# First K and Q projections of the attention moved into the last tile of the first FFN

## The reference, cut to what matters

```
x = L0_attn_x                                # (16, 256, 256) f32
x = x + 0.5 * ffn(layernorm(x), W_up, W_gate, W_down)
x = x + attn(layernorm(x), Wq, Wk, Wv, Wo, head_scale)
x = x + 0.5 * ffn(layernorm(x), W_up, W_gate, W_down)

ffn:  up, gate = x @ wu.T, x @ wg.T          # weights rounded to -1, 0, 1 times a scale, 1024 hidden
      return (silu(up) * gate) @ wd.T
attn: q, k = rotary(x @ Wq), rotary(x @ Wk)  # 16 heads, 4 KV heads of 128, causal
      p = softmax(q @ k.T / sqrt(128))
      return ((p @ v) * head_scale) @ Wo     # 16 sequences of 256 tokens
```

## Time and profile before

| what | us |
|---|---|
| median of 3 runs | 1092.58 |
| lowest and highest of the 3 | 1091.23, 1092.96 |
| the profiled execution | 1092.94 |
| its span in the profile | 1091.1 |
| PE busy in the span | 1070.3 |
| DVE busy in the span | 925.4 |
| ACT busy in the span | 815.4 |
| POOL busy in the span | 713.5 |

### The profile page before, as it was taken

How to read it: one execution, slowest core, us unless ns; L and a number is a source line. 1 busy time by engine, 2 the same in 40 slices (tenths; PEclk the granted TensorE clock), 3 DMA queues, 4 the chain that set the end, 5 groups by cost and what they waited for, 6 DMA issues and landing times.

```text
span 1091.1 us, 26889 instructions
## 1 busy us (share of the span) xinstructions
PE 1070.3 (98%) x8517; PEld 844.1 (77%) x8517; DVE 925.4 (85%) x2313; ACT 815.4 (75%) x2038; POOL 713.5 (65%) x906
## 2 busy tenths in 40 slices
PE   7999999899999999999999999999999999999998
PEld 5556566688888888888888888888888887656565
DVE  6787876899999999999999999999999997433333
ACT  6787887788788787887878878788787785444443
POOL 2566675776777777777777767777677774444443
PEclk9999999999999999999999999999999999999999
DMA  9522332234434344343433434334434343100101
GB/s 347 156 48 40 58 59 37 40 71 89 74 74 76 72 82 82 72 78 65 90 70 72 82 73 81 67 72 82 82 72 76 72 83 73 30 19 19 38 19 38
DMA packets 262166, 79.93 MB, mean 73 GB/s; under 512 B 249328, under 2 KB 260848, under 8 KB 261872
## 3 DMA queue, kind: packets, MB, share of 16 engines
q1 hardware_dynamic: 261696, 79.19, 34.9%
q10 hardware_dynamic: 432, 0.27, 0.1%
HBM read 12.85 MB, written 4.19 MB: 16 GB/s over the span
## 4 chain that ended last, share of the span: by engine, by line
PE 71%; issue 10%; ACT 6%; POOL 6%; DVE 5%; DMA 1%; POOLq 0%; SPq 0%; DVEq 0%; ACTq 0%
PE bank L750 45%; PE bank L808 14%; POOL SCR L409 5%; PE bank L709 4%; PE bank L719 4%; PE bank L739 4%; ACT SCR L619 2%; DVE ARENA L1128 1%; DVE SCR L1089 1%; ACT SCR L492 1%; ACT ARENA L626 1%; DMA X<-in_wg 1%; DVE bank L1108 1%; ACT SCR L507 1%; ACT SCR L517 1%
## 5 line engine op out<-in xcount | busy, mean ns | idle before, releaser
L440 POOL TENSOR_SCALAR SCR<-SCR,RI 128x128 f32<-128x128 f32 (+1 forms) x512 | 309.6, 605 | 44.0 <-DVE RI L1124 3.8
L619 ACT ACTIVATE SCR<-bank,NM 128x128 f32<-128x128 f32 (+1 forms) x512 | 208.2, 419 | 124.3 <-DVE NM L1108 124.3
L425 POOL TENSOR_TENSOR SCR<-SCR 128x512 f32<-128x512 f32 x160 | 203.1, 1269 | 149.4 <-DVE SCR L1089 146.8
L409 POOL TENSOR_TENSOR SCR<-SCR 128x512 f16<-128x512 f32 x128 | 152.7, 1194 | 156.5 <-ACT SCR L507 155.4
L808 PE MATMUL bank<-SCR 128*128 128x128 f32 (+1 forms) x1024 | 193.9, 332 | 4.8 <-ACT SCR L619 4.8
L948 DVE SCALAR_TENSOR_TENSOR SCR<-SCR,CS,bank 128x512 f32<-128x512 f32 x128 | 95.1, 743 | 119.3 <-PE bank L719 98.5
L591 ACT COPY SCR<-bank 64x512 f32<-64x512 f32 x320 | 185.5, 580 | 12.5 <-PE bank L750 6.5
L1128 DVE TENSOR_TENSOR ARENA<-SCR,ARENA 128x768 f16<-128x768 f32 x128 | 187.9, 1468 | 5.5 <-ACT ARENA L626 4.9
L750 PE MATMUL bank<-WOH,ARENA 128*128 128x256 f16 x1024 | 188.3, 273 | 0.8 <-DVE X L1151 0.8
L1108 DVE CUSTOM_DVE_ANT_0 bank<-bank,MASK,SCQ 128x128 f32<-128x128 f32 (+1 forms) x512 | 183.0, 416 | 0.9
L517 ACT ACTIVATE SCR<-bank,SU 128x512 f32<-128x512 f32 x128 | 87.7, 685 | 112.1 <-PE bank L709 110.7
(11 more groups left out here) (120 smaller groups left out, 1651.0 us busy)
## 6 DMA issues: line engine op xcount, KB each, us to landing
out<-X SPq DMA_DIRECT2D x7, 512.0 KB, 2.9
X<-in_x SPq DMA_DIRECT2D x1, 2560.0 KB, 11.2
ARENA<-in_wq SPq DMA_DIRECT2D x1, 2048.0 KB, 13.5
ARENA<-in_wo SPq DMA_DIRECT2D x1, 2048.0 KB, 18.6
SCR<-ARENA SPq DMA_TRANSPOSE x128, 3.6
X<-in_x SPq DMA_DIRECT2D x3, 512.0 KB, 9.9
X<-in_wu SPq DMA_DIRECT2D x2, 512.0 KB, 5.8
X<-in_wg SPq DMA_DIRECT2D x2, 512.0 KB, 7.7
```

The lines of the kernel that those rows point to most:

```text
L409: gp.tensor_tensor(HL[:, f % 4, :], H32[:, f % 2, :], HH[:, f % 4, :], ALU.subtract).then_inc(s["hl_done"], 1)
L425: gp.tensor_tensor(dst, M1[:, m, :], M2[:, m, :], ALU.add).then_inc(add, 1)
L440: last = gp.tensor_scalar(EX[:, par, lo:hi], EX[:, par, lo:hi], RI[:, par, c:c + 1], PS, ALU.mult, ALU.mult)
L619: last = act.activation(EX[:, par, 384 * hh + lo:384 * hh + hi], SBK[hh][:, lo:hi], ACT.Exp, bias=NM[:, par, c:c + 1], scale=-1.0, accum_o ...
```

## The change

K0 and Q0 are projected in the last tile, behind up and gate of pieces 4 and 5, into banks 6 and 7 (`PJ0`). Their swaps follow on ACT in pieces 5 and 6, their multiplications on DVE in pieces 6 and 7; the addition of K0 stands on POOL ahead of piece 7's remainder, that of Q0 behind it. This needs M1 and M2 apart from SG and H32: they go to the addresses of the raw K and V weights, and QF, EX, PT, XN2 and the stores of the second FFN move too. So all casts must be done before the last tile: the fourth quarters of Q, K, V and O move into tiles 4 to 6. The exponential table is loaded ahead of the last `high`. In batch 0, scores of step 0 stand ahead of the Q projection of step 2, the down projections of (7, 5), (7, 6) and (7, 7) go one each into steps 2, 3 and 4, and the residual of tile 7 goes to step 4. The low half of norm job 14 goes to step 0 of batch 0; the job's earlier parts move up by a piece (statistics at piece 2, centering at 4). New waits: the first exponential waits for the last remainder, the first two turns of probabilities for down projections, and values of steps 5 and 6 for the residual.

```
-        CAST_HI = [(2, 2, 5, 6)] * 3 + [(0, 0, 1, 2)]
-        CAST_LO = [(2, 5, 6, 7)] * 3 + [(1, 2, 2, 4)]
+        CASTS_HI = {(4, 2): [(Q, 0), (K, 0)], (4, 5): [(V, 0), (K, 3), (V, 3)], (4, 6): [(O, 0)],
+                    (5, 2): [(Q, 1), (K, 1)], (5, 5): [(V, 1), (Q, 3)], (5, 6): [(O, 1)],
+                    (6, 2): [(Q, 2), (K, 2)], (6, 5): [(V, 2), (O, 3)], (6, 6): [(O, 2)]}
...
-                norm_job(2 * n, n - 1, at + 3, at + 5, at + 5, at + 6)
+                norm_job(2 * n, n - 1, at + 2, at + 4, at + 5, at + FC)
@@ SP, turns of the probabilities
+                            if e < 2:
+                                sp.wait_ge(ff[0]["down_done"], FC * TILES - 1 + e)
@@ POOL, piece
+                if layer == 0 and n == TILES - 1 and f == FC - 1:
+                    rope_add(0, 0, KF[:, 0, :], 0)
                 gp.wait_ge(s["hh_done"], FC * n + f + 1)
@@ ACT, piece
+                    if n == TILES - 1 and f in (5, 6):
+                        act.wait_ge(proj, f - 4)
+                        act.wait_ge(w_ready, 4 * len(CUTS))
+                        rope_swap(f - 5, f - 5, PJ0[f - 5])
@@ ACT, between the FFN and the batches
+            act.activation(WARM[:, 1:2], NEGHALF[:, 0:1], ACT.Exp)
             high(0, TILES - 1, FC - 1)
@@ PE, ffn
-                    if layer == 0 and isinstance(n, int) and (n, f) == (TILES - 1, FC - 1):
-                        pe.wait_ge(w_ready, 3 * len(CUTS) + 2)
-                        pe.wait_ge(ff[0]["silu_done"], FC * TILES - 1)
...
-                        project_qk(PJ[0], WKH, WKL, 0, 0)
+                    if layer == 0 and (n, f) == (TILES - 1, 4):
+                        pe.wait_ge(w_ready, 4 * len(CUTS))
+                        pe.wait_ge(ln_x[1], 16 * (TILES - 2))
+                        project_qk(PJ0[0], WKH, WKL, 0, 0)
+                    if layer == 0 and (n, f) == (TILES - 1, 5):
+                        project_qk(PJ0[1], WQH, WQL, 0, 0)
@@ PE, batch
+                    if first and i == 2:
+                        pe.wait_ge(ff[0]["h_done"], FC * TILES)
+                        scores(0, 0, 0)
...
-                            for f in range(FC - LAG, FC):
-                                down(0, TILES - 1, f)
...
+                    if first and 2 <= i < 2 + LAG:
+                        down(0, TILES - 1, FC - LAG + i - 2)
...
+                        if first and i in (5, 6):
+                            pe.wait_ge(ff[0]["x_done"], SUB * TILES)
@@ DVE, piece
+                    if n == TILES - 1 and f >= FC - 2:
+                        if f == FC - 2:
+                            ve.wait_ge(tab_in, 32)
+                        rope_mul(f - FC + 2, f - FC + 2, PJ0[f - FC + 2])
@@ DVE, batch
+                    if first:
+                        norm_lo(2 * TILES - 2)
...
-                    if isinstance(b, int) and (b, i) == (0, 0):
-
+                    if isinstance(b, int) and (b, i) == (0, 4):
                         residual(0, TILES - 1)
```

More of the change, by code:

```diff
@@ L419, in ffn @@
                     piece(layer, n, f)
[L421 to L425, removed]
             def rows_rstd(e):
@@ L506, in high, with rope_swap @@
                 wait(act, s["down_done"], j - 3)
-                act.copy(HH[:, f % 4, :], H32[:, f % 2, :]).then_inc(s["hh_done"], 1)
+                act.copy(HH[layer][:, f % 4, :], H32[layer][:, f % 2, :]).then_inc(s["hh_done"], 1)
+            def rope_swap(r, m, src):
+                wait(act, add, r - 1)
+                for d, s in ((0, 64), (64, 0)):
+                    last = act.copy(M2[d:d + 64, m, :], src[s:s + 64, :])
+                last.then_inc(swap, 1)
             def piece(layer, n, f):
@@ L583, in _ @@
                 ffn(0, n)
+            act.activation(WARM[:, 1:2], NEGHALF[:, 0:1], ACT.Exp)
             high(0, TILES - 1, FC - 1)
-            def rope_swap(r, m):
-                wait(act, add, r - 1)
-                for d, s in ((0, 64), (64, 0)):
-                    last = act.copy(M2[d:d + 64, m, :], PJ[m][s:s + 64, :])
-                last.then_inc(swap, 1)
             def batch(b):
@@ L597, in batch @@
                     u, t = 2 * b + g, PAIRS * b + i
-                    if real(b, i, 0):
+                    if real(b, i, 0) and not (isinstance(b, int) and b + i == 0):
                         r, m = 5 * u + 1 + k, (5 * g + 1 + k) % 2
@@ L939, in residual, with rope_mul @@
                                             ALU.mult, ALU.add).then_inc(s["x_done"], 1)
+            def rope_mul(r, m, src):
+                wait(ve, add, r - 1)
+                ve.wait_ge(swap, r + 1)
+                two = lambda a: a.rearrange("p (h n) -> p h n", h=2)
+                for dst, a, tb in ((M1[:, m, :], src[:, :], COS), (M2[:, m, :], M2[:, m, :], SIN)):
+                    last = ve.tensor_tensor(two(dst), two(a), tb[:, :].unsqueeze(1).to_broadcast([P, 2, SEQ]), ALU.mult)
+                last.then_inc(mul, 1)
             def piece(layer, n, f, prev):
@@ L988, in weights @@
                     scales()
[L989 to L990 removed]
+                for i, part in CASTS_LO.get((n, f), ()):
                         raw, hi, lo, size, c = CUTS[i]
[L992 to L993 removed]
+                        cols = slice(part * size, (part + 1) * size)
+                        ve.wait_ge(w_hi, HI_ORDER.index((i, part)) + 1)
                         ve.scalar_tensor_tensor(flat(lo)[:, cols], raw[:, cols], AFAC[:, c:c + 1],
@@ L1077, in _ @@
                 ffn(0, n, n > 0)
-            ve.wait_ge(tab_in, 32)
-            def rope_mul(r, m):
-                wait(ve, add, r - 1)
-                ve.wait_ge(swap, r + 1)
-                two = lambda a: a.rearrange("p (h n) -> p h n", h=2)
-                for dst, src, tb in ((M1[:, m, :], PJ[m][:, :], COS), (M2[:, m, :], M2[:, m, :], SIN)):
-                    last = ve.tensor_tensor(two(dst), two(src), tb[:, :].unsqueeze(1).to_broadcast([P, 2, SEQ]), ALU.mult)
-                last.then_inc(mul, 1)
             def batch(b):
@@ L1110, in batch @@
                             last.then_inc(mx, 1)
-                    if real(b, i, 0):
-                        rope_mul(r, m)
-                    if isinstance(b, int) and (b, i) == (0, 0):
+                    if real(b, i, 0) and not first:
+                        rope_mul(r, m, PJ[m])
+                    if isinstance(b, int) and (b, i) == (0, 4):
                         residual(0, TILES - 1)
```

81 lines of the change are left out of this document (38 added, 43 removed).

## The result

| what | before | after |
|---|---|---|
| median of 17 runs each, us | 1092.52 | 1094.87 |
| lowest and highest | 1091.21, 1093.61 | 1093.58, 1095.68 |
| the profiled execution | 1092.94 | 1094.21 |
| its span | 1091.1 | 1092.4 |

The ratio of after to before is 1.0021, 95% interval 1.0015 to 1.0028: 1.6 to 3.1 us slower. The forecast was 1094.2.

A forecast was written before the change was run, and what follows sets the result against it. PE bounds the attention; at the seam its idle time counts, DVE and ACT setting the pace after the first scores. Casts 0, seam 0, clock +1.6 on the median 1092.58 gave 1094.2, range 1090.8 to 1096.0.

The forecast's parts named there:

- The casts: Four more casts in each of tiles 4 to 6, none in tile 7: hidden in ACT's and DVE's slack, 0 us.
- the 1.09 us stall: PE's down projection at 173.29 waits for the residual of tile 6; claimed to go, up of (7, 4) 1.09 earlier.
- s0: Start of the first scores on PE, released by POOL's addition of Q0: forecast 192.15, before 194.65.
- one such collision: DVE's low half of norm job 14 overlapping a POOL remainder ahead of the first scores: POOL loses 0.9 us.
- From s0 to the mark: From first scores to maxima of step 3, with Q2 and tile 7's residual on the path: 18.8 us, 16.3 before.
- The seam at the full clock: From the first FFN's last tile to the maxima of step 3, without a clock fall: 0 us change.
- The clock: PE's pause of 4.5 us ahead of the first scores drops the clock to 1.2 GHz: +1.6 us.
- the row at 15 to 20 us: Profile window with a PE pause of 1.79 us; up and gate took 3.35 instead of 1.73, source of the 1.6.
- the clock didn't hold: Rival: the clock holds through PE's pause and the seam is a wash, 1092.6 (1091.7 to 1093.7); chance 0.27.
- the lead didn't come through: Rival: shorter DVE and ACT path behind the first scores keeps their lead, 1090.1 to 1091.1; chance 0.13, 0.04 for more.
- the slower mechanism: Rival: three POOL collisions, first scores at 193.2, they and Q2 at half speed: +1.1 + 2.7 = 3.8, 1096.4; chance 0.11.
- the casts hid: Rival claimed the opposite: casts make PE wait in tiles 4 to 6, 3 x 1.24 less 1.1, 1095.2; chance 0.05.

The follow-up runs named there:

- e7: Kernel before with only the casts moved into tiles 4 to 6 and PE's wait before the first K projection for all casts; ratio to before 0.9984.
- e8: Changed kernel with DVE's low half of norm job 14 behind the rotary products of Q1 instead of ahead of them; ratio to before 1.0002.
- e4: Changed kernel with POOL's addition of Q0 ahead of the remainder of (7, 7) instead of behind it; ratio to before 1.0002.
- e1: Changed kernel with 20 unread identity matmuls on PE in the pause between the first Q1 projection and the first scores; ratio to before 1.0007.
- e10: e2 with 14 unread identity matmuls on PE in the pause between Q2 and the first scores; ratio to before 0.9986.
- e2: Changed kernel with Q2 projected on PE ahead of the first scores instead of behind them; ratio to before 1.0000.
- e3: Changed kernel with down projections of (7, 5) and (7, 6) ahead of the first scores, Q2 still behind; median 1094.48 us, ratio to before 1.0007.
- e5: Changed kernel with down (7, 5), Q2 and down (7, 6) ahead of the first scores, Q0's addition ahead of the last remainder; 1089.80 us, ratio to before 0.9967.
- e6: e5 with the residual of tile 7 at step 3 and the last down projection right behind the first scores; 1089.58 us, ratio to before 0.9966.

## Why the prediction was right, and where its sizes were off

**The casts cost nothing: right.** No wait in tiles 4 to 6, and the 1.09 us stall gone. What I had missed is that they are worth 0.87 us more in the old arrangement (e7), 0.65 of it because the K projection, by the reading above, waited for a silu that came late behind ACT's norm work. The changed kernel has no use for it, since K0 goes to a bank of its own.

**s0: too early by 0.68.** Forecast was 192.15 - 162.94 = 29.21 from up of (7, 0), it came at 29.89. The step that failed is "I take one such collision, 0.9": there were three. Against 1.27 alone, K0's addition took 1.72; the last remainder 2.13 against 1.16; and Q0's addition 1.71. That is 1.8 us in all, 0.9 more than the forecast had, and all of it stands ahead of s0. The steps without collisions were put about 0.3 too long together: e8, with K0's collision of 0.4 left, has s0 at 28.46, where the forecast without any is 191.25 - 162.94 = 28.31. So the whole change brings s0 forward by 1.82 us, no more than the casts alone do (1.95): the early K0 and Q0 gave nothing, because Q0's addition stood in POOL's queue. e4 shows what was to be had, 1.55 us, by one line's place.

**From s0 to the mark: 18.16 at the full clock (e1), forecast 18.8.** The first part, from s0 to the first low probabilities, was right: 10.13 us in e1, forecast 10.0. With Q2 ahead of s0 (e10) it is 8.32, so Q2's place costs 1.8 us, where the forecast had 10.0 - 8.53 = 1.5. The second part, from there to the mark, is the term that was too large: 7.77 before, put at 8.81 with the residual in it, and 212.77 - 204.73 = 8.04 in after. So the residual was put at 1.04 us and costs 0.27. Its 1.57 us filled the wait of 0.54, and the low probabilities behind it took 0.92 instead of 1.48; POOL's addition that ran beside them before has ended here when they start. That this made them shorter was not tested by itself.

The two errors, s0 0.68 too late for the forecast and the way to the mark 0.64 too short, cancel. That is luck: one comes from POOL's queue, the other from DVE's waits. The seam at the full clock came out at +0.07, forecast 0.

**The clock: +1.6 forecast, 1.69 measured** (e1 against after), for the reason given: at 1.2 GHz s0 and Q2 take 197.29 - 192.92 = 4.37 us, where before they take 2.73. The pause was 5.00 us, forecast 4.5. The mechanism was right; that the size of the row at 15 to 20 us (1.6) fits to 0.1 us is in part luck, since it comes from other instructions, and how much of s0 and Q2 would run at the lower clock was left between 0 and 2.7 us. The Trainium skill (TensorE: Matmul & The Clock Gate, Why this matters for your kernels) warns of long idle gaps between bursts of matmuls; the trace of after agrees, with a granted clock of 0.73 behind the 5.00 us. In the 17 runs of after the mean clock was never above 0.997.

**The sum.** By the mark +1.73 us, by the medians +2.35, with an interval that holds the first. I can't place the 0.6 between them: the lowest times of the two kernels, 1093.58 and 1091.21, also lie 2.4 apart, and how the starts (below) and the fall at the pause combine in the timed runs, no trace shows. The forecast's case came true. At +2.35 us it lies at the 2.2 us that the prediction took as the least that a measurement can tell, and its interval is clear of zero. The rivals: the clock didn't hold in the profiled execution; the lead didn't come through, since s0 had less of it; the slower mechanism was half there, with all three collisions but with s0 at 29.9 instead of 30.3, and with 1.7 instead of its 2.7 for the clock; the casts hid.

## What to carry to other kernels

When work is moved to an earlier place, follow its result through the queue of every engine up to the one that consumes it: here PE and DVE had Q0 ready, and one remainder ahead of it on POOL, with the collisions, ate the gain. An order that leaves TensorE a pause of several microseconds can pay for it again behind the pause (1.7 us here), so put ready matmuls into it, enough to close it (two down projections alone were too few; with a projection between them and the addition earlier, it closed); and what is put behind a critical matmul instead of ahead of it is paid in full if the next engine needs it. A change made of several parts should be timed by its parts: the casts alone brought the mark forward by 1.96 us, and the rest of this change moved it back by 3.69.

## What the runs showed of the hardware

**A pause of the same length can cost or not.** With 3.50 us idle the clock held in the profiled run of e2. In eight of its ten others the mean clock was 0.993 to 0.995, lower than in any run of e7 or e10, which have no such pause (0.996 and more), so there it fell. With 3.44 and 3.57 it fell in the profiled runs of e4 and e8; with 3.27 it fell in the profiled run of e3 and seems to have held in three of twelve; with 5.00 it fell in the profiled run of after, and none of its 17 runs has a mean clock above 0.997. So a single profile doesn't show what such a pause costs; a median can.

**The start of the kernel.** PE's timeline of e7 behind 18 us, where the first up and gate run at full speed:

```profile
18.34 1.02 PE L715 MATMUL bank<-XX,TU 128*128 128x512 f16 x4
19.20 1.03 PE L725 MATMUL bank<-XX,TG 128*128 128x512 f16 x4
```

and of e5, which has the same code there:

```profile
18.55 1.87 PE L717 MATMUL bank<-XX,TU 128*128 128x512 f16 x4
20.21 1.91 PE L727 MATMUL bank<-XX,TG 128*128 128x512 f16 x4
```

In the earlier trace rows two groups run at half speed, here none or several. The runs of e7 fall into 1090.02 to 1090.52 us at a mean clock of 1.000 and 1092.07 to 1092.88 at 0.996 to 0.997, with one between: I take this to be a good part of the spread that every kernel here has, 1.5 us in e6 to 4.5 in e3, and it is why I compared seams from up of (7, 0).
